# Latent attention: the values of a pair of heads in four runs, with five buffers of probabilities

## The reference, cut to what matters

```python
Wdkv = x @ latent_w + latent_b                      # [4, 1024, 36]
q = einsum('btc,hcl->bhtl', x, Wd_w) + Wd_b          # 16 heads of 36
scores = einsum('bhtl,bsl->bhts', q, Wdkv) / sqrt(8)
scores = where(causal, scores, -inf)
attn = softmax(scores, axis=-1)
y = einsum('bhts,bsl->bhtl', attn, Wdkv)             # values: the same latent
z = y.transpose(0, 2, 1, 3).reshape(b, t, 16 * 36)
return z @ out_w + out_b
```

## Time and profile before

| | |
|---|---|
| times of three runs | 3430.93, 3431.35, 3438.45 us; median 3431.35 |
| the profiled execution's span | 3431.1 us, 60614 instructions |
| TensorE (matmul) busy | 3037.7 us, 89% |
| VectorE busy | 2268.8 us, 66% |
| ScalarE busy | 1317.9 us, 38% |
| GpSimd busy | 765.6 us, 22% |
| first and last copy into yT | 2332.5 and 3286.2 us |

### The profile page before, as it was taken

How to read it: one execution, slowest core, us unless ns; L and a number is a source line. 1 busy time by engine, 2 the same in 40 slices (tenths; PEclk the granted TensorE clock), 3 DMA queues, 4 the chain that set the end, 5 groups by cost and what they waited for, 6 DMA issues and landing times. The chain is left out here.

```text
span 3431.1 us, 60614 instructions
## 1 busy us (share of the span) xinstructions
PE 3037.7 (89%) x18088; PEld 2189.2 (64%) x18088; DVE 2268.8 (66%) x5128; ACT 1317.9 (38%) x2660; POOL 765.6 (22%) x1073
## 2 busy tenths in 40 slices
PE   5999999787777877769999999779989989999987
PEld 4777777565555555547777777446666666666653
DVE  6777777587786877857777777345555555555533
ACT  2111111266665765641111111225545545545532
POOL 1323232154354444422323232000000000000000
PEclk9999999888998888979999999779999999999998
DMA  3000000000000000011000000000000000000000
GB/s 121 0 0 0 0 0 0 1 2 2 3 3 3 2 2 2 2 63 35 0 0 0 0 0 0 1 0 1 1 2 1 1 2 1 1 2 1 1 1 25
DMA packets 13037, 24.17 MB, mean 7 GB/s; under 512 B 2306, under 2 KB 7682, under 8 KB 12804
## 3 DMA queue, kind: packets, MB, share of 16 engines
q1 hardware_dynamic: 12804, 21.22, 1.9%
HBM read 18.52 MB, written 2.10 MB: 6 GB/s over the span
## 5 line engine op out<-in xcount | busy, mean ns | idle before, releaser
L555 DVE SCALAR_TENSOR_TENSOR moe_acc<-moe_ps,moe_comb,moe_acc 128x512 f32<-128x512 f32 x896 | 661.7, 745 | 174.0 <-PE moe_ps L304 170.9
L1335 DVE SCALAR_TENSOR_TENSOR attn_R<-attn_R 128x512 f32<-128x512 f32 (+1 forms) x592 | 478.5, 864 | 115.5 <-ACT attn_R L1221 115.1
L1910 DVE TENSOR_REDUCE attn_mx<-attn_psm 128x1 f32<-128x128 f32 (+7 forms) x512 | 369.3, 754 | 243.0 <-PE attn_psm L1642 242.4
L1820 ACT ACTIVATE attn_probs<-attn_pse 128x512 f32<-128x512 f32 (+1 forms) x640 | 323.4, 553 | 330.1 <-PE attn_pse L1655 263.6
L304 PE MATMUL moe_ps<-moe_Wg,moe_xh 128*128 128x512 f32 x1024 | 328.8, 403 | 24.2 <-DVE moe_Wu L501 24.2
L1221 ACT ACTIVATE attn_R<-attn_ps 128x512 f32<-128x512 f32 (+1 forms) x640 | 321.2, 568 | 64.9 <-PE attn_ps L1079 64.8
L335 PE MATMUL moe_ps<-moe_Wd,moe_ih 128*128 128x512 f32 x1024 | 338.0, 411 | 0.0
L304 PE MATMUL moe_ps<-moe_Wu,moe_xh 128*128 128x512 f32 x1024 | 337.1, 411 | 0.0
L1671 PE MATMUL attn_psy<-attn_probs,attn_V 128*64 128x128 f32 (+3 forms) x2304 | 317.7, 397 | 0.1
L1079 PE MATMUL attn_ps<-attn_qS,attn_kM 128*128 128x128 f32 (+3 forms) x1152 | 263.9, 372 | 45.9 <-issue 43.2
L1079 PEld LDWEIGHTS attn_ps<-attn_qS,attn_kM 128*128 128x128 f32 x1152 | 210.1, 228 | 109.9 <-issue 60.0
(11 more groups left out here) (207 smaller groups left out, 5302.4 us busy)
## 6 DMA issues: line engine op xcount, KB each, us to landing
moe_stageg<-in_w_gate SPq DMA_DIRECT2D x8, 512.0 KB, 6.8
moe_stageu<-in_w_up SPq DMA_DIRECT2D x8, 512.0 KB, 7.5
moe_stageg<-in_w_down SPq DMA_DIRECT2D x8, 512.0 KB, 3.6
out<-X SPq DMA_DIRECT2D x1, 2048.0 KB, 8.7
attn_qS<-attn_mh SPq DMA_DIRECT2D x64, 4.0 KB
attn_qS<-attn_ml SPq DMA_DIRECT2D x64, 4.0 KB
attn_wd<-in_wd SPq DMA_DIRECT2D x1, 864.0 KB, 5.5
attn_w<-in_wqkv SPq DMA_DIRECT2D x1, 768.0 KB, 5.1
```

Source lines behind the costliest of these rows:

```text
L555: dve.scalar_tensor_tensor(acc[:, q, r, :], expert_bank[j % 4][:, :], comb[:, q, r, e:e + 1], acc[:, q, r, :], ALU.mult, ALU.add).then_inc ...
L1335: dve.scalar_tensor_tensor(r, r, -SLOPE, r, ALU.add, ALU.mult).then_inc(u_ready, 1)
L1820: act.activation(probs[:, u % 2, c, HALF - n:HALF], e_bank[c][:, HALF - n:HALF], ACT.Exp, scale=SCORE_SCALE).then_inc(p_ready, 1)
L1910: dve.reduce_max(mx[:, q, v:v + 1], m_all[:, base:base + (v % 8 + 1) * P], AX.X).then_inc(mx_ready, 1)
```

## The change

The probabilities get five buffers (`RING`), and `values` takes a group of units: units 0 to 2, 3 to 5, 6 and 7, 8 and 9. The first group stands behind the scores (and maxima) of unit 3, the second behind those of unit 6, the third behind those of unit 8, and the fourth behind the scores of unit 0 of the next pair, ahead of its maxima; in the last pair of an element it stands at the pair's end. `y_ready` is gone: `pv_ready` counts groups, four in a pair. The copy of the upper half into `yT` moves with the fourth group, on ScalarE behind the exps of the next pair's unit 0. `MAXIMA` deals the maxima out otherwise. The first two pairs of an element are written out ahead of the loop, which then runs over the two middle iterations.

```diff
-        probs = sb("probs", [P, 2, 2, HALF])
+        probs = sb("probs", [P, RING, 2, HALF])
...
+        TOGETHER = ((0, 1, 2), (3, 4, 5), (6, 7), (8, 9))
+        NG = len(TOGETHER)
+        GROUP_OF = [g for g, us in enumerate(TOGETHER) for _ in us]
+        AFTER = {3: 0, 6: 1, 8: 2}
...
-                with eng.Fori(0, PAIRS // 2 - 1) as i:
+                for i in range(2):
+                    pair(b * PAIRS + i, i, i, b, (True, True))
+                with eng.Fori(1, PAIRS // 2 - 1) as i:
...
-        MAXIMA = (range(0, 4), range(4, 6), range(6, 7), range(7, 9), range(9, 12), range(12, 14), range(14, 16))
+        MAXIMA = (range(0, 2), range(2, 5), range(5, 8), range(8, 9), range(9, 12), range(12, 15), range(15, 16))
...
-                def values(m, q, u):
-                    s, pieces = units[u]
...
-                    last.then_inc(y_ready if end else pv_ready, 1)
+                def values(m, g):
+                    for u in TOGETHER[g]:
+                        s, pieces = units[u]
+                        first = u in (0, NQ0)
+                        if first:
+                            pe.wait_ge(yc_ready, after(m * 2 + s - 1))
+                        pe.wait_ge(p_ready, after(m * 2 * NU + 2 * u + 1))
+                        end = u in (NQ0 - 1, NU - 1)
+                        for k, (kt, at_, qc, n, _) in enumerate(pieces):
+                            for c in range(2):
+                                last = pe.matmul(y_bank[VW * c:VW * (c + 1), qc:qc + n], V[:, kt, :], probs[:, u % RING, c, at_:at_ + n],
+                                                 start=first and k == 0, stop=end, skip_group_check=True)
+                    last.then_inc(pv_ready, 1)
...
                     for u in range(NU):
                         scores(m, q, u)
+                        if u == 0 and not first_pair:
+                            values(m - 1, NG - 1)
...
-                        if u >= 1:
-                            values(m, q, u - 1)
+                        if u in AFTER:
+                            values(m, AFTER[u])
...
-                    values(m, q, NU - 1)
+                    if last_pair:
+                        values(m, NG - 1)
...
-                    act.wait_ge(y_ready, after(m * 2 + s))
+                    act.wait_ge(pv_ready, after(m * NG + (NG - 1 if s else 0)))
...
+                                if u < RING:
+                                    act.wait_ge(pv_ready, after((m - 1) * NG + GROUP_OF[u + NU - RING]))
                                 else:
-                                    act.wait_ge(pv_ready, after(m * (NU - 2) + (u - 2) - (1 if u - 2 >= NQ0 else 0)))
+                                    act.wait_ge(pv_ready, after(m * NG + GROUP_OF[u - RING]))
...
+                        if u == 0 and not (isinstance(i, int) and i == 0):
+                            copy_out(m - 1, i - 1, 1)
...
-                    copy_out(m, i, 1)
+                    if isinstance(i, int) and i == PAIRS - 1:
+                        copy_out(m, i, 1)
```

More of the change, by code:

```diff
@@ L1416 @@
 PAIRS = HEADS // 2
+RING = 5
 STACK = 3 * LAT
@@ L1491, in attn1_phase @@
             sem("sm_ready"), sem("mx_ready"), sem("mt_ready"), sem("mh_ready"), sem("ml_ready"), sem("m_in"))
-        s_ready, p_ready, pv_ready, y_ready, yc_ready = (
-            sem("s_ready"), sem("p_ready"), sem("pv_ready"), sem("y_ready"), sem("yc_ready"))
+        s_ready, p_ready, pv_ready, yc_ready = sem("s_ready"), sem("p_ready"), sem("pv_ready"), sem("yc_ready")
         zt_ready, r_ready, z_ready, zz_ready, zc_ready, o_ready = (
@@ L1569, in take_over @@
                     pool.wait_ge(s_ready, after(b * PAIRS * 2 * NU - 1))
-                    pool.wait_ge(y_ready, after(b * PAIRS * 2 - 1))
+                    pool.wait_ge(pv_ready, after(b * PAIRS * NG - 1))
                     pool.sem_inc(pool_pause, 1)
@@ L1587, in _ @@
             def _(pe):
-                for s in (xt_ready, kp_ready, vp_ready, qp_ready, sm_ready, mt_ready, s_ready, pv_ready, y_ready,
+                for s in (xt_ready, kp_ready, vp_ready, qp_ready, sm_ready, mt_ready, s_ready, pv_ready,
                           zt_ready, zz_ready, o_ready):
@@ L1689, in pair @@
                 def pair(m, q, i, b, ahead):
-                    last_pair = isinstance(i, int) and i == PAIRS - 1
+                    first_pair, last_pair = isinstance(i, int) and i == 0, isinstance(i, int) and i == PAIRS - 1
                     pe.wait_ge(m_in, (m + 1) * 64)
@@ L1811, in pair @@
                             if c == 0:
[L1813 to L1816, removed]
+                                if u < RING:
+                                    act.wait_ge(pv_ready, after((m - 1) * NG + GROUP_OF[u + NU - RING]))
                                 else:
-                                    act.wait_ge(pv_ready, after(m * (NU - 2) + (u - 2) - (1 if u - 2 >= NQ0 else 0)))
+                                    act.wait_ge(pv_ready, after(m * NG + GROUP_OF[u - RING]))
                             n = 256 if len(units[u][1]) == 1 and units[u][1][0][3] == 256 else HALF
-                            act.activation(probs[:, u % 2, c, HALF - n:HALF], e_bank[c][:, HALF - n:HALF], ACT.Exp,
+                            act.activation(probs[:, u % RING, c, HALF - n:HALF], e_bank[c][:, HALF - n:HALF], ACT.Exp,
                                            scale=SCORE_SCALE).then_inc(p_ready, 1)
+                        if u == 0 and not (isinstance(i, int) and i == 0):
+                            copy_out(m - 1, i - 1, 1)
                         if ahead[0] and u == NU - 2:
```

## The result

The changed kernel takes 3459.03 us (median of four runs, 3455.67 to 3464.02) against 3431.14 for the kernel before (one run more than before, four now, 3425.93 to 3438.45): ratio 1.0078, 95% interval 1.0058 to 1.0097. It is slower by 0.8%, 28 us. The forecast was 3457.5 and slower. The profiled execution has a span of 3453.9 us, 22.8 more than before.

What follows compares the result with a forecast made beforehand. TensorE's instruction order was taken to bound a pair. An ordinary pair changes by -1.70 + 1.7 + 1.0 = +1.0 us, +27.0 over 27 pairs; with the other pairs +26.2, giving 3457.5 us, range 3426 to 3477.

Steps and rivals of the forecast that it cites:

- the walk: Start times forecast step by step through a changed ordinary pair, counted from scores(0): scores(3) at 8.5 us, scores(4) at 12.3.
- Term 1: TensorE's switches between whole-array matmuls and value runs: five round trips fewer at 0.34 us, -1.70 us a pair.
- Term 2: Maxima in a row on TensorE wait for VectorE's reduces: 2.5 us in place of 0.8, +1.7 us a pair.
- scores(8) behind scores(7): With no values between them, scores(8) waits for unit 7's exps to free the score banks: +1.0 us a pair.
- the ring: Five probability buffers: exp of unit u waits for the run holding unit u-5, which ended before in every case; no cost.
- the moved copy: Upper-half copy into yT behind the next pair's unit 0 exps: takes 0.6 us, done by 4.2, hidden.
- the DMA: Brings the row of maxima before the next pair's start: slack of 1.1 us all used up, cost 0, upper end 0.3.
- (a): Pairs on the way back in the loop: values of units 8 and 9 cover the table load, 6 x -0.32 = -1.9 us.
- (b): Seventh pair in three elements: units 0 to 2 cover TensorE's 1.81 us wait at maximum 11; -1.15 each, -3.4 in all.
- (c): Last element, pairs seven and eight together: fewer round trips against added waits and uncovered values, sum +4.5 us.
- Rival 3: TensorE's clock falls to 1.2 GHz for a stretch in each of 27 pairs, about 1.5 us each: 3498 us, chance 0.08.
- Rivals 1 and 2: First: VectorE keeps up, no added maxima waits, 3405 us, chance 0.12. Second: half the waits don't come, 3433 us, chance 0.08.

Runs made afterwards that it cites:

- split_runs: Changed kernel with two added one-column whole-array matmuls in pairs two to seven, inside the runs of units 0-2 and 3-5: a pair 0.55 us above split_control.
- short_before: Kernel before the change with each maximum reduced over its own 128 columns only: an ordinary pair falls by 0.27 us, to 26.33.
- short_after: Changed kernel with each maximum reduced over its own 128 columns only: an ordinary pair falls by 1.60 us, to 25.89.
- six_late: Kernel before the change with unit 6's values moved to unit 7's, five buffers and first pairs written out: a pair of 27.24 us against 26.59.
- even_grouped: Kernel before the change with maxima dealt 3, 2, 2, 2, 2, 2, 2, 1, values in eight runs, first two pairs written out: 3392.41 us, ratio 0.9883.
- six_back: Changed kernel with unit 6's values back behind scores(7) in a run of their own: a pair of 27.95 us against 27.49.
- unrolled: Kernel before the change with only the first two pairs of an element written out: no pair of 26.93 us left, six table loads gone.
- first_pair: Changed kernel with the old dealing of maxima in each element's first pair only: first to second transpose 24.96 us in place of 30.76.
- split_control: Changed kernel with two added one-column whole-array matmuls in pairs two to seven, ahead of the runs of units 0-2 and 3-5: a pair of 27.47 us.
- even_maxima: Kernel before the change with only the maxima dealt 3, 2, 2, 2, 2, 2, 2, 1 behind units 0 to 7: 3409.25 us, ratio 0.9934.

## Why the prediction was right, by its steps

The time came out 1.5 us above the forecast, inside the range. That it is so near is in part luck: the old kernel's median alone was 3431, 3433 and 3437 in three sets of runs, and below stand costs that no term had. The ordinary pair came out at +0.89 for +1.0, and its rows stand within 0.1 us of the walk. By terms:

| step | forecast, us a pair | measured | by |
|---|---|---|---|
| 1, five round trips fewer | -1.70 | about -1.4 | rows below, split_runs |
| 2, waits for the reduces | +1.7 | +1.33 to +1.40 | short_before, short_after; the held starts |
| 3, scores(8) behind scores(7) | +1.0 | +0.99 | six_late |
| sum | +1.0 | +0.9 to +1.0 | |
| the pair | +1.0 | +0.89 | |

*Term 1* was too large by 0.3, and term 2 by 0.3 to 0.4; the errors cancelled. Four of the five removed ways out of a run stood ahead of scores, and after the change these scores follow a mask matmul of the maxima. There the weight load isn't hidden either. scores(2) takes 0.33 behind a run in the earlier trace rows's pair and still 0.32 behind the mask (2411.09 to 2411.41 above), where I had counted 0.24:

```profile
2407.64 0.50 PE L1655 MATMUL attn_pse<-attn_qS,attn_kS 110*128 110x256 f32 x2
2407.97 0.57 PE L1639 MATMUL attn_psm<-attn_kS,attn_qS 108*128 108x512 f32 x2
```

From start to start the first matmuls of scores(3), scores(5) and scores(6) shrink as little, from 0.50 to 0.48, 0.34 to 0.33 and 0.58 to 0.55. So of the 0.34 some 0.08 stay in four places: 1.70 - 0.32 = 1.38. With the measured 1.33 and 0.99 the sum is +0.94 for 0.89. even_grouped agrees: the round trip that it has less, ahead of scores that follow a mask, is worth 0.27. With short reduces it is -1.38 + 0.99 = -0.39, measured -0.44. That the load is what stays is argued from these rows and from the 0.27 of split_runs; no kernel removed the load alone.

*Term 2* was mis-sized in the new order's waits, 2.5 in the forecast. In the new pair the six held starts sum to 2.2 (0.48 + 0.40 + 0.31, then 0.40, 0.31, 0.30 at maxima 11, 13 and 14). The old order's 0.8 was right (0.79), which makes 1.40. The walk had the starts right and the same work without waits too short: scores(2), for one, was counted at 0.24 and takes 0.32. What it takes more was booked as a wait in term 2 and as a saving in term 1, so part of the cancelling is no luck. (The 0.23 a matmul that the walk takes from six in 1.47 is 0.245; it moves nothing, scores(3) came at 8.42 for 8.5.)

*Costs nothing*: the ring, the moved copy and the DMA did cost nothing in an ordinary pair, as said. six_back shows how near the last of them was.

*The others*, from the distances between transposes. (a) 1.9 us in six places did go, and unrolled shows why: the mechanism that I gave, cover by units 8 and 9, was wrong; writing the pairs out removed the loads, and whether units 8 and 9 would have covered them was not put to the test. (b) In the seventh pairs the wait of 1.81 is gone, and the stretch up to the next transpose falls from 28.19, 29.73 and 31.11 to 27.50 in all three. The last two owe more than my 1.15 to the clock, which had been at its lower level for 3.4 and 6.8 us of them (2750.2 to 2753.6 and 3006.2 to 3013.0) and no longer is. (c) From the last transpose to the last copy into yT it is now 3282.6 to 3309.4, 26.8, and was 3262.6 to 3286.2, 23.6: +3.2. With the 0.9 ahead of that transpose it is 4.1 of the +4.5.

*Rival 3* came in small. Ordinary pairs kept the upper level with 2.2 us of waits for the reduces in each. The Trainium skill (TensorE: Matmul & The Clock Gate, "A second HAM failure mode: psum-queue depth-cycling") tells of a kernel in which frequent small idles between groups of matmuls made the clock swing; the ordinary pairs here do not bear this out. In the first pair of the first element the clock did fall:

```profile
2324.60:2334.80 10.20, 10.14 (x49) 7.30 (x50) 4.39 (x5) 1.85 (x4) 0.00 (x0) 0.50 0.00 0
```

With 10.2 us at 1.2 GHz this pair is 5.1 us longer than in the kernel before and 5.8 longer than in first_pair. Between the elements the three stretches with `finish` grew too: the first from 60.48 to 62.80 us at a clock of 0.86 in place of 0.89, the others from 59.89 to 63.37 and from 51.78 to 52.90 (0.9 of each growth is a pair's). The cause is open; it is not the dealing in the first pairs, since first_pair has 62.9, 62.5 and 52.2 there. These costs were in no term.

All in all, by the distances between transposes in the two profiled executions: +5.1 in the first pair, +16.8 in 21 ordinary ones, -6.5 and +0.1 in the stretches up to and behind the seventh transpose of the first three elements, +6.9 in those with `finish`, together +22.4. Beyond an ordinary pair's 0.9 the first pair and `finish` cost some 8.4, and the seventh pairs gained some 6 more than forecast; these nearly cancel, and that was luck.

*Rivals 1 and 2*: VectorE didn't keep up. What rival 1 supposed is what short_after built, and there the order did win.

## What to carry to other kernels

Work that looks like a nuisance between two instructions can be the cover for another engine's answer: before merging short runs on the bottleneck engine, write down for each pair of instructions that become neighbours which buffer ties them and how long its answer takes. A walk from start times (not from modelled durations), with the one wait rule of the two-deep buffer, placed ten starts in a pair of 27.5 us within 0.1 us. And where an engine's order feeds two others (here VectorE with maxima and ScalarE with scores), deal the work out evenly first: one line in `MAXIMA` brought 0.7%, and merging only where no cover was lost another 0.5%, together with the first pairs written out.

## What the runs showed of the hardware

- Going from whole-array matmuls to column tiles of 64 and back cost 0.27 us with a bf16 matmul of one column in between (split_runs against split_control), 0.27 for one run less ahead of scores that follow a mask (even_maxima to even_grouped), and 0.34, by the distances in the earlier trace rows, where the next scores start straight behind the run.
- Two score matmuls of 256 columns took 0.32 us from start to the next start behind a 128-column bf16 matmul and 0.33 behind a switch. That it is the weight load of 128 fp32 columns that is exposed in both is argued, not shown.
- ScalarE's table load (1.28 us) came once for each iteration of the loop over pairs in the three elements inside the loop over the batch, nine times; not at all in the last element, which has the same loop outside of it; and once for each of the three with the first two pairs written out. One cost 0.32 us in the old order and 0.8 in even_maxima.
- TensorE's clock stayed at 2.4 GHz through pairs with six waits of 0.3 to 0.5 us and one of some 0.6 (scores(8)). It fell to 1.2 for 10.2 us in the first element's first pair, after a wait of 1.05, and stayed at 2.4 in the last element's first pair, which lacks that wait.
